# Two-layer cross-attention with gated feed-forward: the second attention layer's tiles taken two at a time, its layer norm cut into quarters

## The chip, the core and the metric

The kernel runs on one core of one Trainium2 chip. The metric is the device time of one execution in microseconds (us), as the median of a few runs. The engines are TensorE (PE in the rows; its weight loads are PEld), VectorE (DVE), ScalarE (ACT), GpSimd (POOL) and SyncE (SP), which issues every DMA here.

## The reference, cut to what matters

A model of two layers works on x of shape (32, 56, 256): 32 batches of 56 tokens. Each layer is a layer norm, a cross-attention over a context of (32, 1500, 64), a second layer norm and a feed-forward part (a mixture of 16 experts with a shared one in layer 0, a pair of routed low-rank corrections in layer 1). The change is in the attention of layer 1, which in the reference is

```python
q_hk = (hidden_q @ Wq.T).reshape(b, s, H, K)            # H = 16 heads, hidden_q = layernorm(x)
q_big = jnp.einsum('bshk,hkq->bshq', q_hk, w_kc_q)
kv_rope = kv_c * cos[None] + _rotate_half(kv_c) * sin[None]
q_r = jnp.einsum('bshq,hqr->bhsr', q_big, W_qr)
k_r = jnp.einsum('bld,hdr->bhlr', kv_rope, W_kr)
scores = jnp.einsum('bhsr,bhlr->bhsl', q_r, k_r)        # l runs over 1500 keys
attn = jax.nn.softmax(scores, axis=-1)
ctx_c = jnp.einsum('bhsl,bld->bhsd', attn, kv_rope)
ctx_lat = jnp.einsum('bhsd,hkd->bshk', ctx_c, w_kc_kv)
out = ctx_lat.reshape(b, s, H * K) @ Wo.T
```

All of it is in float32. The rotated keys depend only on the context, so layer 1 reads them from memory, where layer 0 left them.

## The kernel before

**Tiles.** The products of weights are formed once at the start of the program. In attention, a batch has 16 x 56 = 896 pairs of head and token, held as two halves of 448 columns: heads 0 to 7 on partitions 0 to 63, heads 8 to 15 on partitions 64 to 127. The 1500 keys are 12 tiles of 125. Batches go in four groups of eight (`g` is the group, `j` the batch in it, `b` = 8g + j, `t` the tile). One layer norm, one set of queries and one output projection serve a group.

**Work of one tile.** Four kinds of step make up nearly all of it.

- `score` (L953 to L963): four matmuls for each half, 64 rows deep, 125 columns of keys, 448 streamed: high parts of keys and queries, low part of the keys, low part of the queries, and a rank-one matmul (L963) that subtracts the row maximum, which lies in `shift`. They fill a wide region of PSUM (0 or 1, by turns). ScalarE then takes the exponential (L1075) into one of four buffers of `prob`.
- `mix` (L977): `prob` times the values, 125 rows deep, 64 columns for each half, two passes each, added over the 12 tiles into region 2.
- The sum of the exponentials over the tiles: GpSimd adds tiles 0 to 10 into `sums` in ten 125x896 additions (L1135), in the step `mix` of tiles 1 to 10. Step `context` adds tile 11 on VectorE (L1256). In the very last batch GpSimd takes tiles 0 to 6 only and VectorE the rest (L1243).
- `smax` (L937): the maxima for a batch still to come. They need no low parts: two halves of 500 keys against 112 queries fill region PAIR, and VectorE reduces it to its maxima (L1222). PAIR is one buffer, so a maximum's matmuls wait for the reduction of the maximum before. There are twelve a batch, four tiles ahead (`EARLY_MAX`).

**Work of one batch.** `maxneg` (L1229) negates the finished maxima, `maxT` (L943, L1062) transposes them, and SP moves them into `shift` (L861) for the next batch's scores. `norm` (L984) sums the exponentials of the batch before over its keys, ScalarE copies them out (L1088), SP packs them (L843), `spread` takes the reciprocals (L1262) and SP spreads them (L847, L852); `share` (L1286) multiplies the mixed values by them. `fetch` (L820, L822) loads the keys and values of the batch after the next. `project` (L1012) is the output projection of the group before, in batch j = 1.

**Layer norm of the next group.** `mean` (L883), `square` (L1176), `var` (L889, root on ScalarE at L1027), `rstd` (reciprocal L1181 and product L1183, in two halves of 224 columns), `xsplit` (high part on ScalarE L1033, remainder on VectorE L1188): all in batch j = 5. The eight `query` steps (six full-array matmuls, L872 to L874; L1055 and L1217 split the result) follow in batch j = 6.

**Order.** `rolling_schedule` writes one list of steps. Each engine walks through this list and executes its own part of every step, in the list's order, waiting on semaphores; SP's DMAs are issued in the same order. So the place of a step in the list is its place in every engine's queue. Before the change the order in a tile is

```python
add("score", b, t, region=t % 2)
add("mix", *old)                 # tile t - 1
if ahead[0] < NB:
    maximum(*ahead)              # four tiles ahead
```

with the steps of the batch and of the group placed between by the value of `t`. Layer 0 has a schedule of its own.

## Time and profile before

| | us |
|---|---|
| median of 3 runs | 3165.96 |
| lowest and highest run | 3162.75, 3173.43 |
| the profiled execution | 3168.89 |
| its span, from first to last instruction | 3167.1 |
| first score to last mix of the second attention layer | 963.8 |

The profile is of one execution. A window is a stretch of its span, counted in us from the span's start; busy times in it are those of each engine, and PEclk is the clock that TensorE was granted, as a share of 2.4 GHz. In a timeline the columns are start, length, engine, line of the kernel, operation, what is written and read, sizes and count; in brackets the engine's idle time before it and what ended that. Neighbouring instructions of one kind are merged, and then the length runs from the first start to the last end.

### The profile page before, as it was taken

How to read it: one execution, taken by the hardware profiler on the slowest of the kernel's cores; microseconds unless marked ns; L12 is line 12 of the kernel's file. 1: busy time of each engine (PE TensorE's matmuls, PEld its weight loads, DVE VectorE, ACT ScalarE, POOL GpSimd, SP SyncE). 2: the span in 40 equal slices, each digit the busy share in tenths (PEclk: the TensorE clock that was granted, in tenths of full speed). 3: DMA queues.
4: the chain of work that ended last, by engine and by line, in shares of the span. 5: the costliest groups of instructions: out<-in, count | busy, mean ns of one | idle time of the engine just before them, and what ended most of it. 6: DMA issues, size and time to landing. Idle time of an engine off the chain costs nothing. (4 is left out here: it accounts for less than half of the span.)

```text
span 3167.1 us, 42548 instructions
## 1 busy us (share of the span) xinstructions
PE 2853.3 (90%) x15928; PEld 1633.2 (52%) x15928; DVE 1954.6 (62%) x2322; ACT 1177.4 (37%) x1640; POOL 1668.3 (53%) x935
## 2 busy tenths in 40 slices
PE   7689899999998999996899889999999999986898
PEld 6444444444544454443788744444454454445665
DVE  2576667666766676655666556655665655636664
ACT  2124441444144423442333234444443443433331
POOL 0467775776677776771200047677676666742111
PEclk8689999999999999997899989999999999997998
DMA  8333331333133322322000143232323232300000
GB/s 288 109 84 75 87 92 34 88 76 104 36 76 84 92 58 62 75 52 85 1 1 1 28 89 80 66 78 63 75 63 75 63 75 63 83 30 23 7 6 12
DMA packets 98836, 209.15 MB, mean 66 GB/s; under 512 B 30306, under 2 KB 74322, under 8 KB 91116
## 3 DMA queue, kind: packets, MB, share of 16 engines
q1 hardware_dynamic: 98636, 206.44, 25.1%
q8 instruction: 131, 2.15, 0.3%
q14 instruction: 69, 0.57, 0.1%
HBM read 135.36 MB, written 46.00 MB: 57 GB/s over the span
## 5 line engine op out<-in xcount | busy, mean ns | idle before, releaser
L1135 POOL TENSOR_TENSOR sums<-sums,prob 125x896 f32<-125x896 f32 x556 | 1176.1, 2115 | 285.2 <-ACT prob L1075 242.2
L1222 DVE TENSOR_REDUCE maxpart<-pair 112x2 f32<-112x1000 f32 x744 | 889.9, 1196 | 451.8 <-PE pair L937 451.3
L1075 ACT ACTIVATE prob<-wide 125x896 f32<-125x896 f32 x768 | 704.4, 917 | 903.0 <-PE wide L963 901.1
L977 PE MATMUL single<-prob,kv 125*64 125x448 f32 x3072 | 753.8, 569 | 0.5
L958 PE MATMUL wide<-qhigh,kparts 64*125 64x448 f32 x3072 | 448.7, 369 | 1.5 <-DVE maxpart L1222 1.5
L937 PE MATMUL pair<-kparts,qhigh 64*112 64x500 f32 x1488 | 360.7, 481 | 88.0 <-DVE maxpart L1222 86.5
L937 PEld LDWEIGHTS pair<-kparts,qhigh 64*112 64x112 f32 x1488 | 130.1, 171 | 520.6 <-DVE maxpart L1222 440.0
L1135 POOL TENSOR_TENSOR sums<-prob 125x896 f32<-125x896 f32 x64 | 135.1, 2111 | 362.2 <-ACT prob L1075 362.2
L958 PEld LDWEIGHTS wide<-qhigh,kparts 64*125 64x125 f32 x3072 | 281.7, 184 | 79.6 <-issue 48.2
L963 PE MATMUL wide<-shift,ones_row 64*125 64x448 f32 x1536 | 284.5, 365 | 3.9 <-DMA shift<-maxrow 3.9
L958 PE MATMUL wide<-qlow,kparts 64*125 64x448 f32 x1536 | 283.0, 363 | 0.0
L977 PEld LDWEIGHTS single<-prob,kv 125*64 125x64 f32 x3072 | 152.7, 135 | 239.4 <-issue 234.9
L1096 POOL TENSOR_TENSOR w_low<-w_low_values,w_high 128x384 fp32r<-128x384 f32 (+1 forms) x72 | 74.8, 1044 | 280.1 <-ACT w_high L1038 280.1
L1120 POOL TENSOR_TENSOR sums<-prob 96x448 f32<-96x448 f32 x128 | 145.8, 1159 | 46.6 <-issue 24.0
L1864 POOL TENSOR_TENSOR ffn_hsum<-ffn_hid 128x448 f32<-128x448 f32 (+1 forms) x24 | 29.6, 1232 | 250.9 <-DVE ffn_hid L1990 250.9
L963 PEld LDWEIGHTS wide<-shift,ones_row 64*125 64x125 f32 x1536 | 144.7, 183 | 19.4 <-DMA shift<-maxrow 6.6
L958 PEld LDWEIGHTS wide<-qlow,kparts 64*125 64x125 f32 x1536 | 144.2, 183 | 13.4
L1286 DVE TENSOR_TENSOR ctx_n<-ctx_raw,recip 128x448 f32<-128x448 f32 x62 | 88.6, 1430 | 61.1 <-DMA recip<-zrec_merged 61.1
L872 PE MATMUL wide<-x_high,w_high 128*96 128x448 f32 (+1 forms) x272 | 105.9, 390 | 20.4 <-POOL w_low L1096 12.4
L1193 DVE TENSOR_TENSOR kparts<-single,kparts 64x500 fp32r<-64x500 f32 x94 | 63.0, 670 | 97.4 <-ACT kparts L1045 97.4
L1055 ACT ACTIVATE qhigh<-single 128x448 fp32r<-128x448 f32 (+3 forms) x80 | 32.0, 431 | 225.0 <-PE single L919 192.0
L1344 PE MATMUL wide<-moe_x_high,moe_wexp_high 128*128 128x448 f32 x272 | 107.8, 396 | 6.9 <-DVE moe_hid L1597 6.4
(329 smaller groups left out, 3898.2 us busy)
## 6 DMA issues: line engine op xcount, KB each, us to landing
kparts<-keys_merged SPq DMA_DIRECT2D x64, 750.0 KB, 8.9
kparts<-kparts SPq DMA_DIRECT2D x96, 250.0 KB, 3.1
keys_merged<-kparts SPq DMA_DIRECT2D x32, 750.0 KB, 7.3
recip<-zrec_merged SPq DMA_DIRECT2D x124, 112.0 KB, 2.8
w_low_values<-w_merged SPq DMA_DIRECT2D x64, 192.0 KB, 2.4
raw<-in_ctx SPq DMA_DIRECT2D x32, 375.0 KB
values_merged<-kv SPq DMA_DIRECT2D x32, 375.0 KB
kv<-values_merged SPq DMA_DIRECT2D x32, 375.0 KB
```

The costliest lines, as they stand in the source:

```text
L872: pe.matmul(dst, w_hi, x_hi, start=start, stop=False)
L937: mm = pe.matmul(acc[0:TQ, half, 0:LB], qhigh[rows_of(half), b % slots, t * TQ:(t + 1) * TQ], kparts[rows_of(half), b % 3, 0, third * LB:( ...
L958: pe.matmul(acc[0:LP, half, 0:HQ], kparts[rows_of(half), b % 3, part, cols], q[rows_of(half), b % slots, :], start=(i == 0), stop=False)
L963: mm = pe.matmul(acc[0:LP, half, 0:HQ], c["ones_row"][rows_of(half), 0:LP], shift[rows_of(half), b % 2, :], start=False, stop=True)
L977: mm = pe.matmul(mix_acc[64 * half:64 * half + DC, 0:HQ], kv[:, b % 3, t, :], prob[:, (b * LT + t) % NPROB, half * HQ:(half + 1) * HQ], st ...
L1075: nc.scalar.activation(prob[:, n_ % NPROB, :].rearrange("p (a b) -> p a b", a=2), acc[0:LP, :, 0:HQ], ACT.Exp)\
L1096: nc.gpsimd.tensor_tensor(w_low[:, h % HSLOT, :, :], w_in[:, h % HSLOT, :, :], w_high[:, h % HSLOT, :, :].bitcast(F32), ALU.subtract)\
L1120: nc.gpsimd.tensor_tensor(qr[:, h % 4, half, :], qa[:, h % 2, half, :], qb[:, h % 2, 1 - half, :], ALU.add)\
L1135: nc.gpsimd.tensor_tensor(dst, first_in, prob[:, n_ % NPROB, :], ALU.add).then_inc(s["pool_sum"], 1)
L1222: V.tensor_reduce(maxpart[:, b % 2, t:NMAX:4, third], acc[0:TQ, :, 0:LB], AX.X, ALU.max).then_inc(*R.signal_drained(kind, *key))
L1286: V.tensor_tensor(ctx_n[:, b % BG, :], ctx_raw[:, b % 2, :], recip[:], ALU.mult).then_inc(s["ctx_ready"], 1)
L1344: pe.matmul(dst, w_hi, x_hi, start=start, stop=False)
```

## The change

The second layer's schedule goes through pairs of tiles (`p` is the pair, t = 2p). In a pair the order becomes: maximum, score t, score t + 1, maximum, mix t - 2, mix t - 1. The mixes lie two tiles behind the scores, and two of them are left over after the last batch.

- Both maxima use the same region PAIR as before, the two scores regions 0 and 1.
- A query stands behind each of the two maxima, in batch j = 6, pairs 0 to 3.
- `fetch` is at the beginning of pair 1, ahead of `norm`, which is at that pair's end. `context` is at the end of pair 0, `spread` at the end of pair 3, `share` at the end of pair 5. `maxneg` is ahead of the second maximum of pair 4, `maxT` behind it.
- `project` is at the ends of pairs 2, 3 and 4, the last of them with two halves.
- The layer norm begins a batch earlier: `mean`, `square` and `var` in batch j = 4 (pairs 2, 3 and 5). In batch j = 5 the reciprocals come in four quarters of 112 columns at the ends of pairs 0 to 3 (`invert`), the products in four quarters behind the first maximum of pairs 1 to 4 (`scale`), the high part in pair 4, and the remainder in two halves in pair 5 (`xrest`), one behind the first maximum and one at the end.
- Ahead of the first batch the same quarters and halves are used. Layer 0 keeps halves (`NORM_PARTS`, `REST_PARTS`).

```diff
+NORM_PARTS = (2, 4)
+REST_PARTS = (1, KT)
...
+    def ahead(b, t):
+        n = t + EARLY_MAX
+        due = (b + 1, n) if n < LT else (b + 2, n - LT)
+        if due[0] < NB:
+            maximum(*due)
...
-    for part in range(2):
-        add("rstd", 0, part)
+    for part in range(NORM_PARTS[1]):
+        add("invert", 0, part)
+        add("scale", 0, part)
     add("xsplit", 0)
+    for k in range(KT):
+        add("xrest", 0, k)
...
-        for t in range(LT):
-            ahead = (b + 1, t + EARLY_MAX) if t + EARLY_MAX < LT else (b + 2, t + EARLY_MAX - LT)
-            if t == 2 and b + 2 < NB:
+        following = g + 1 < G
+        for p in range(LT // 2):
+            t = 2 * p
+            queries = following and j == BG - 2 and p < NPAIR // 2
+            if p == 1 and b + 2 < NB:
                 add("fetch", b + 2)
-            add("score", b, t, region=t % 2)
-            if b + 1 < NB and t == 8:
+            ahead(b, t)
+            if queries:
+                add("query", g + 1, t, region=3)
+            if following and j == BG - 4 and p == 3:
+                add("square", g + 1, 0)
+            if following and j == BG - 3 and 1 <= p <= 4:
+                add("scale", g + 1, p - 1)
+            if following and j == BG - 3 and p == 5:
+                add("xrest", g + 1, 0)
+            add("score", b, t, region=0)
+            add("score", b, t + 1, region=1)
+            if b + 1 < NB and p == 4:
                 add("maxneg", b + 1)
-            if t or b:
-                old = (b, t - 1) if t else (b - 1, LT - 1)
-                add("mix", *old)
-                if not t:
+            ahead(b, t + 1)
+            if b + 1 < NB and p == 4:
+                add("maxT", b + 1, region=3)
+            if queries:
+                add("query", g + 1, t + 1, region=3)
+            if p or b:
+                old = (b, t - 2) if p else (b - 1, LT - 2)
+                add("mix", old[0], old[1])
+                add("mix", old[0], old[1] + 1)
+                if not p:
                     add("context", b - 1)
-            if t == 1 and b:
+            if p == 1 and b:
                 add("norm", b - 1, region=3)
-            if b + 1 < NB and t == 9:
-                add("maxT", b + 1, region=3)
-            if g and j == 1 and t in (2, 3, 5, 6):
-                m, half = divmod((2, 3, 5, 6).index(t), 2)
-                add("project", g - 1, m, half, region=None if half else 3)
+            if g and j == 1 and 2 <= p <= 4:
+                for m, half in (((0, 0),), ((0, 1),), ((1, 0), (1, 1)))[p - 2]:
+                    add("project", g - 1, m, half, region=None if half else 3)
...
-            if g + 1 < G and j == BG - 2 and t < NPAIR:
-                add("query", g + 1, t, region=3)
-            if ahead[0] < NB:
-                maximum(*ahead)
-            if t == 8 and b:
+            if p == 3 and b:
                 add("spread", b - 1)
-            if t == 10 and b:
+            if p == 5 and b:
                 add("share", b - 1, 2)
+    add("mix", NB - 1, LT - 2)
     add("mix", NB - 1, LT - 1)
...
+                elif kind == "invert":
+                    g, part = key
+                    cols = slice(part * NT // norm_parts, (part + 1) * NT // norm_parts)
+                    dve.wait_ge(*R.drained("var", g))
+                    V.reciprocal(x_rstd[:, cols], x_std[:, cols]).then_inc(s["rstd"], 1)
+                elif kind == "scale":
+                    g, part = key
+                    cols = slice(part * NT // norm_parts, (part + 1) * NT // norm_parts)
+                    dve.wait_ge(s["rstd"], norm_parts * g + part + 1)
+                    V.tensor_tensor(x_n[:, :, cols], x_cen[:, :, cols], x_rstd[:, cols].unsqueeze(1).broadcast_to([128, KT, NT // norm_parts]), ALU.mult)\
+                        .then_inc(s["normed"], 1)
+                elif kind == "xrest":
+                    g, k = key
+                    dve.wait_ge(s["x_high"], g + 1)
+                    V.tensor_tensor(x_low[:, k, :], x_n[:, k, :], x_high[:, k, :].bitcast(F32), ALU.subtract).then_inc(s["x_low"], 1)
```

## Rows read from the trace of the kernel before

**Rows 1.** The page, part 1: busy time of each engine, share, instructions

```profile
PE 2853.3 (90%) x15928; PEld 1633.2 (52%) x15928; DVE 1954.6 (62%) x2322; ACT 1177.4 (37%) x1640; POOL 1668.3 (53%) x935
```

**Rows 2.** Busy time by stretch: the layer, then batches 3, 5, 6, 9, 31

```profile
1858.60:2822.40 963.80, 934.13 (x5794) 463.12 (x5794) 563.41 (x577) 420.23 (x537) 666.58 (x316) 0.99 0.28 68
1939.40:1966.34 26.94, 26.54 (x176) 13.06 (x174) 16.62 (x16) 12.34 (x15) 21.05 (x11) 1.00 0.34 82
...
1993.22:2030.00 36.78, 30.26 (x184) 14.42 (x182) 27.70 (x26) 16.39 (x19) 22.33 (x11) 1.00 0.25 60
2030.00:2068.97 38.97, 37.93 (x224) 21.44 (x222) 20.76 (x33) 17.19 (x31) 21.11 (x10) 1.00 0.23 56
2122.38:2162.14 39.76, 39.36 (x208) 18.85 (x206) 18.00 (x19) 12.34 (x15) 21.52 (x11) 1.00 0.23 55
...
2797.70:2822.40 24.70, 24.59 (x154) 10.83 (x152) 5.94 (x7) 12.22 (x15) 14.36 (x7) 1.00 0.03 10
```

**Rows 3.** Timeline of one tile, the last of batch 22

```profile
2567.63 0.48 PE L937 MATMUL pair<-kparts,qhigh 64*112 64x500 f32 x2
...
2567.95 0.57 PE L958 MATMUL wide<-qhigh,kparts 64*125 64x448 f32 x4
2568.15 1.20 DVE L1222 TENSOR_REDUCE maxpart<-pair 112x2 f32<-112x1000 f32 x1 [0.93 <-PE pair L937]
...
2568.55 0.37 PE L963 MATMUL wide<-shift,ones_row 64*125 64x448 f32 x2
...
2568.85 0.97 PE L977 MATMUL single<-prob,kv 125*64 125x448 f32 x4
2568.96 0.92 ACT L1075 ACTIVATE prob<-wide 125x896 f32<-125x896 f32 x1 [1.21 <-PE wide L963]
...
2569.76 0.48 PE L937 MATMUL pair<-kparts,qhigh 64*112 64x500 f32 x2
```

**Rows 4.** Timeline of TensorE, batch 1: a mix, a normaliser (between), a maximum

```profile
1889.03 0.97 PE L977 MATMUL single<-prob,kv 125*64 125x448 f32 x4
...
1890.68 0.48 PE L937 MATMUL pair<-kparts,qhigh 64*112 64x500 f32 x2
```

**Rows 5.** Waits in the layer: in total, times, longest

```profile
PE pair L937 <- DVE maxpart L1222: 26.6, 34, 2.6
```

**Rows 6.** Timelines of VectorE, GpSimd and ScalarE at the start of batch 3

```profile
1940.43 1.19 DVE L1222 TENSOR_REDUCE maxpart<-pair 112x2 f32<-112x1000 f32 x1
1941.54 1.08 DVE L1256 TENSOR_TENSOR sums<-prob,sums 125x896 f32<-125x896 f32 x1
...
1943.99 2.11 POOL L1135 TENSOR_TENSOR sums<-prob 125x896 f32<-125x896 f32 x1 [3.97 <-ACT prob L1075]
1946.88 8.83 POOL L1135 TENSOR_TENSOR sums<-sums,prob 125x896 f32<-125x896 f32 x4 [0.78 <-ACT prob L1075]
...
1943.00 0.92 ACT L1075 ACTIVATE prob<-wide 125x896 f32<-125x896 f32 x1 [1.14 <-PE wide L963]
```

**Rows 7.** Timelines of VectorE and GpSimd in batch 5, around a layer norm's products

```profile
2014.33 1.54 DVE L1181 RECIPROCAL x_std<-x_std 128x224 f32<-128x224 f32 x1
2015.91 2.51 DVE L1183 TENSOR_TENSOR x_n<-x_cen,x_std 128x448 f32<-128x448 f32 x1
...
2021.34 0.62 DVE L1183 TENSOR_TENSOR x_n<-x_cen,x_std 128x448 f32<-128x448 f32 x1
...
2015.86 2.08 POOL L1135 TENSOR_TENSOR sums<-sums,prob 125x896 f32<-125x896 f32 x1
```

**Rows 8.** Timeline of TensorE in batch 6: a query's first matmul, the maximum behind it

```profile
2040.35 0.47 PE L872 MATMUL single<-x_high,w_high 128*128 128x448 f32 x1
...
2041.77 0.48 PE L937 MATMUL pair<-kparts,qhigh 64*112 64x500 f32 x2
```

**Rows 9.** Timeline of SP's queue, batch 3: the fetch's first issues

```profile
1946.98 1.13 SPq L820 DMA_DIRECT2D kparts<-keys_merged  x2
```

**Rows 10.** DMA from 1939 to 1967, busy tenths in 40 slices of 0.7 us

```profile
DMA  0000000000000949998999913333100100001420
```

More of the change, by code:

```diff
@@ L126, in rolling_schedule @@
                     add("context", b - 1)
-            if t == 1 and b:
+            if p == 1 and b:
                 add("norm", b - 1, region=3)
-            if b + 1 < NB and t == 9:
-                add("maxT", b + 1, region=3)
-            if g and j == 1 and t in (2, 3, 5, 6):
-                m, half = divmod((2, 3, 5, 6).index(t), 2)
-                add("project", g - 1, m, half, region=None if half else 3)
-            if g + 1 < G and j == BG - 3:
-                if t == 2:
+            if g and j == 1 and 2 <= p <= 4:
+                for m, half in (((0, 0),), ((0, 1),), ((1, 0), (1, 1)))[p - 2]:
+                    add("project", g - 1, m, half, region=None if half else 3)
@@ L136, in rolling_schedule @@
+            if following and j == BG - 4:
+                if p == 2:
                     add("mean", g + 1, region=3)
-                if t in (3, 4):
-                    add("square", g + 1, t - 3)
-                if t == 5:
+                if p == 3:
+                    add("square", g + 1, 1)
+                if p == 5:
                     add("var", g + 1, region=3)
-                if t in (7, 8):
-                    add("rstd", g + 1, t - 7)
-                if t == 10:
+            if following and j == BG - 3:
+                if p < NORM_PARTS[1]:
+                    add("invert", g + 1, p)
+                if p == 4:
@@ L144, in rolling_schedule @@
                     add("xsplit", g + 1)
-            if g + 1 < G and j == BG - 2 and t < NPAIR:
-                add("query", g + 1, t, region=3)
-            if ahead[0] < NB:
-                maximum(*ahead)
-            if t == 8 and b:
+                if p == 5:
+                    add("xrest", g + 1, 1)
+            if p == 3 and b:
                 add("spread", b - 1)
-            if t == 10 and b:
+            if p == 5 and b:
                 add("share", b - 1, 2)
+    add("mix", NB - 1, LT - 2)
@@ L751, in attention @@
     mix_acc = region[2]
+    norm_parts, rest_parts = NORM_PARTS[layer], REST_PARTS[layer]
     steps = attention_schedule(layer)
@@ L899, in _ @@
                     pe.wait_ge(s["w_low"], NW * g + h + 1)
-                    pe.wait_ge(s["x_low"], g + 1)
+                    pe.wait_ge(s["x_low"], rest_parts * (g + 1))
                     for half in range(2):
@@ L922, in _ @@
                         pe.wait_ge(s["w_low"], h + 1)
-                        pe.wait_ge(s["x_low"], g + 1)
+                        pe.wait_ge(s["x_low"], rest_parts * (g + 1))
                         for k in range(KT):
@@ L1025, in _ @@
                     if g:
-                        act.wait_ge(s["normed"], 2 * g)
+                        act.wait_ge(s["normed"], norm_parts * g)
                     nc.scalar.activation(x_std[:], acc[:, 0:NT], ACT.Sqrt, bias=c["eps"][:, 0:1]).then_inc(*R.signal_drained(kind, *key))
@@ L1029, in _ @@
                     g, = key
-                    act.wait_ge(s["normed"], 2 * (g + 1))
+                    act.wait_ge(s["normed"], norm_parts * (g + 1))
                     if g:
@@ L1173, in _ @@
                         dve.wait_ge(s["x_high"], g)
-                        dve.wait_ge(s["x_low"], g)
+                        dve.wait_ge(s["x_low"], rest_parts * g)
                     dve.wait_ge(*(R.drained("mean", g) if k == KT - 1 else (s["cen_half"], g + 1)))
@@ L1184, in _ @@
                         .then_inc(s["normed"], 1)
-                elif kind == "xsplit":
+                elif kind == "invert":
[13 more added lines that the diff above has]
+                    V.tensor_tensor(x_low[:, k, :], x_n[:, k, :], x_high[:, k, :].bitcast(F32), ALU.subtract).then_inc(s["x_low"], 1)
+                elif kind == "xsplit" and layer == 0:
                     g, = key
```

## The prediction

> **What bounds the kernel now.** I began with the page: TensorE is busy for 90% of the span, VectorE for 62%, GpSimd for 53% [rows 1]. Only the second attention layer is edited, so the next view is the busy time by stretch. From its first score to its last mix this layer takes 963.8 us for 32 batches; TensorE is 97% busy in it, at a granted clock of 0.99 to 1.00 of the 2.4 GHz level [rows 2]. The reader should compare a plain batch (26.94 us) with those that carry the layer norm (36.78), the queries (38.97) and the output projection (39.76).
>
> Busy is not full, so the third view is the timeline of one undisturbed tile. The maximum begins at 2567.63, the score 0.32 us later, the mix 0.90 after that, the next maximum 0.90 after that: 2.13 us a tile [rows 3]. The score is four steps of two halves side by side; the last starts 0.60 to 0.61 behind the first, so together they stream for 0.81, and for 0.09 of the 0.90 nothing does. A lone mix also takes 0.90, but a mix with the normaliser behind it (same shapes, same passes) takes 1.65 [rows 4]: the normaliser costs 0.75, 0.373 a pass, with no gap, so 0.15 of a lone mix is gap. The maximum streams 500 columns where a score step has 448, hence 0.23 of its 0.32, with 0.09 of gap. The score follows the maximum (both 64 rows deep) with no more than that; the gaps stand where the shape changes to the mix's 125x64 or back. They add up to 0.34 us a tile. The last batch, which has no maxima, agrees: its 24.70 us are 12 x (0.81 + 0.75 + 0.34) + 0.75 and 1.1 of tail [rows 2].
>
> The waits view confirms that VectorE doesn't bound this: in the whole layer the maximum's matmuls wait 26.6 us for it [rows 5], and in the plain tile the reduction ends at 2569.35, 0.4 before the next maximum [rows 3].
>
> **The order.** A round is now maximum A, score, score, maximum B, mix, mix. It streams for 2 x (0.226 + 0.812 + 0.746) = 3.57 and has one pair of shape changes: 3.91, against 4.25 for two tiles before. Score behind score, maximum behind score and mix behind mix are not in the trace; each seam lies between 0 (the normaliser behind the mix, the score behind the maximum) and 0.15 (the lone mix). I take 0, since the shape stays. A's reduction starts 0.52 behind A and lasts 1.20 [rows 3], to 1.72; B's turn comes at 0.32 + 1.62 = 1.94. With its weights already loaded, B streams 0.09 sooner: reduced from 2.37 to 3.57, and the next A comes at 3.91. VectorE is left with two free places in a round, of about 0.7 and 0.85 us. Two exponentials of 0.92 fit, and prob's four buffers come free a round ahead.
>
> **The context sum.** This decides the size. Before, the 125x896 sum of L1256 ran at 1941.54, while GpSimd was idle until 1943.99, and took 1.08 [rows 6]. Now it stands behind B's reduction in a batch's first round and issues at 2.37 + 1.11 = 3.48 (1.11 lies between the two VectorE starts of [rows 6]). GpSimd's first sum needs the exponential of tile 1: the score's last step at 0.93, the exponential 0.41 later [rows 3], two of 0.92 make 3.17 at the latest, and GpSimd starts 0.07 behind it [rows 6]: 3.24. GpSimd is first, by 0.24. What follows the trace shows: a VectorE product with both inputs in SBUF, issued 0.05 after a GpSimd sum began, took 2.51 us, to 0.48 after that sum's end; alone it took 0.62 [rows 7]. So the context sum, which likewise needs all but 0.14 of its length afterwards, ends at 3.24 + 2.10 + 0.94 = 6.3. Behind it waits the next A's reduction (data at 4.43; now 6.22 to 7.42), behind that the second round's B, which loads at 7.47 and streams at 7.56, not at 3.91 + 1.94 = 5.85: 1.71 lost.
>
> A batch without collision is 6 x 3.91 + 0.75 (normaliser) + 0.19 (the transposed maxima, two passes of 0.373 x 112/448) = 24.40; a plain one becomes 26.11. The 26.94 before are 12 x 2.13 + 0.94 and 0.44 of waiting.
>
> The Trainium skill (SBUF — State Buffer, Who interferes with whom) says that such a pair excludes each other for the whole instruction and that the order of issue decides who blocks. The trace agrees in [rows 7]; with the order turned, its rule gives the first rival below.
>
> The normalised share (0.62 alone) issues 3 x 3.91 + 0.19 + 3.48 = 15.40 us after the third round begins. GpSimd's sums then come every 2.24 us (8.83 less 2.10, over 3 [rows 6]) from 2.33 on; the sixth of them ends at 15.6, so the share waits 0.2 and fits. If it lost a whole sum, the context sum would come later and wait that much less: the same total.
>
> **Layer norm.** Mean and variance are four full-array passes each: 4 x 0.373 + 0.20 (shape changes) = 1.69. They move to batch 4 of a group, where I add 0.6 for the two subtractions ahead of A's reduction and 0.5 for a square that meets GpSimd: 26.11 + 3.4 + 1.1 = 30.6. Then the square root's table loads push the first exponentials of batch 5 past 3.48, so its context sum goes first, and quarter 0's reciprocal behind it costs 0.7: a quarter lies between half and all of the 1.54 that 224 columns take [rows 7], and I take 0.84, near the half, because it has half the columns. The quarter products (half of 0.62 and a start, 0.35) stand behind A's reduction in the place of 0.7: alone they fit, behind a GpSimd sum they don't. By the 2.24 beat that costs 0.3, 0.6 and 0.15 around quarters 1 and 2, and 1.2 for quarter 3, behind which wait the maxima's negation and, on TensorE, its transpose. 24.40 + 2.95 = 27.35. Both batches: 57.95, against 26.94 + 36.78 = 63.72: 5.8 saved, three times. Bounds: 55 with no collision, 63 with each product and remainder a whole sum late.
>
> **Queries, projection, ends.** A query between mix and maximum costs 1.42 [rows 8]: six steps of 0.203 and 0.20 of shape changes. A round now has two, with three shape changes more than it has without them: 2 x 1.22 + 0.6 = 3.04, four times. 24.40 + 12.2 = 36.6, the context sum having room in rounds of 7 us: 2.4 saved, three times. Projection: 32 passes of 0.373 and three changes, 12.6, and 0.2 for its additions: 38.9, 0.86 saved, three times. Batch 0 has no context sum: 2.1 saved. Batch 30 loses its maxima after four rounds: 0.8. In batch 31 the last score starts after 5 x 3.46 + 0.75 + 0.9 = 18.95 us, not 11 x 1.90 + 0.75 = 21.65, and the VectorE chain behind it stays: 2.7. Ahead of batch 0, four short reciprocals and products stand for two long: 0.3 lost.
>
> **SP's queue.** A batch's fetch now stands ahead of the normaliser's small transfers, before behind them. The fetch issued at 1946.98 [rows 9] keeps the engines busy until about 1959.3 [rows 10], 12.3 us. Now it issues at 4.0 and is done at 16.3; the small transfer issues at 10.9. It lands between 13 (nothing in its way) and a little past the fetch's end; I take the later, 17. Its reader, the short reciprocal, issues at 17.7 and may wait until 18.6 before it delays a reduction: no cost. Each us past that costs one in 29 batches.
>
> The Trainium skill (DMA: Bandwidth & Descriptors, Queues, rings and completion order) says that an engine takes a ring's descriptors in order, which speaks for the later end. No row here shows the two in this order.
>
> **Sum.** Plain 17 x 0.83 = 14.1; layer norm 17.3; queries 7.1; projection 2.6; ends 5.6 less 0.3: 46. The profiled execution took 3168.9, 1.8 more than its span of 3167.1, and lies 2.9 above the median; 3122.5 by its time, 3120 against the median.
>
> **Rivals.** (1) The context sum issues first, or GpSimd's comes 0.25 later. For it: a margin of 0.24 out of five durations; against: these repeat from tile to tile. 1.6 comes back in 24 batches: 3082. 16%. (2) More collisions: shares, products and remainders lose whole sums, since GpSimd is now busy for 22.4 of 26 us. Half to one and a half us a batch: 3136 to 3165. 15%. (3) Slower: the gap belongs to every step whose first load carries a wait, not to the shape. For: each gap stands at such a load; against: the score behind the maximum and the normaliser behind the mix carry one too. Then 192 x 0.34 = 66 is not saved while the collisions remain: 3186; from 0.24 us of seams a round on it decides. 7%. (4) The small transfer lands later than 18.6: slower from 1.6 us beyond; 3178 at 2 us. 7%.
>
> **Numbers.** The forecast has 55%, 3106 to 3136, likeliest 3120. Low 3076 takes in (1), high 3150 most of (2): some 80%. Under 0.3% (9.5 us) a change can't be told from none. Faster: 55 + 16 + 11 of (2), 82%; within: 4 of (2) and 3 of (4), 7%; slower: 11%.
>
> **What would show it.** Eight mix matmuls in a row and rounds of 3.91; half as many idle loads ahead of the mix; L1256 at a mean near 2.6 us, with a wait of 1.7 ahead of a maximum in each second round; plain batches of 26.1, batches 5 and 6 of a group at 27.4 and 36.6. I am wrong if L1256 stays at 1.08, if score behind score shows a gap, or if the short reciprocal waits for its transfer.

## The result and the profile after

The changed kernel takes 3080.16 us (median of 4 runs, 3079.88 to 3087.07) against 3164.36 (4 runs, 3161.05 to 3173.43): a ratio of 0.9735, 95% interval 0.971 to 0.9759, 84 us less. That lies inside the range, 40 us under the likeliest value, and 2 us from the first rival (3082): the context sum is not held up by GpSimd. The page's busy times, to be read against [rows 1]:

```profile
PE 2786.6 (91%) x15928; PEld 1666.3 (54%) x15928; DVE 1952.0 (63%) x2342; ACT 1155.3 (38%) x1640; POOL 1717.0 (56%) x935
```

The busy time by stretch, as in [rows 2] (length, then busy time and instructions of PE, PEld, DVE, ACT, POOL, granted clock, DMA): the layer, then batches 2, 4, 5, 6, 9 and 31, each from its first score to the next batch's. The layer's window and that of batch 31 end at 2735.90, short of the last mix, whose row (four mixes merged) stands below them.

```profile
1856.02:2735.90 879.88, 870.24 (x5786) 499.87 (x5788) 559.17 (x592) 397.97 (x537) 715.77 (x316) 1.00 0.31 75
1907.32:1931.92 24.60, 24.60 (x177) 14.19 (x174) 16.34 (x17) 11.60 (x15) 22.68 (x11) 1.00 0.37 89
1956.92:1985.56 28.64, 28.32 (x184) 15.51 (x182) 18.69 (x20) 13.09 (x17) 25.52 (x11) 1.00 0.31 76
1985.56:2013.60 28.04, 26.31 (x182) 15.22 (x178) 23.90 (x26) 14.27 (x18) 22.88 (x11) 1.00 0.33 79
2013.60:2049.62 36.02, 35.48 (x217) 21.76 (x218) 22.27 (x33) 16.46 (x31) 20.90 (x11) 1.00 0.25 61
2098.52:2135.76 37.24, 37.24 (x208) 20.07 (x206) 17.42 (x19) 11.60 (x15) 24.29 (x11) 1.00 0.25 59
2714.26:2735.90 21.64, 21.64 (x152) 11.99 (x152) 7.63 (x7) 11.59 (x14) 16.50 (x8) 1.00 0.04 12
...
2734.23 3.23 PE L1005 MATMUL single<-prob,kv 125*64 125x448 f32 x16
```

The last mix ends at 2737.46, so from its first score to its last mix the layer takes 881.4 us where it took 963.8: 82.4 less, nearly the whole gain. The remaining 2 us are less than what the stretches ahead of the layer and behind it differ by among runs with the same code there. A plain batch takes 24.6 instead of 26.94. The six rounds of batch 1, read from the starts of the scores, are 3.92, 4.66 (with the normaliser), 3.93, 3.92, 4.11 (with the transposed maxima) and 3.93. A round of batch 3 on TensorE's timeline, beside the tile of [rows 3]:

```profile
1944.10 0.48 PE L965 MATMUL pair<-kparts,qhigh 64*112 64x500 f32 x2
1944.42 0.57 PE L986 MATMUL wide<-qhigh,kparts 64*125 64x448 f32 x4
...
1945.23 0.58 PE L986 MATMUL wide<-qhigh,kparts 64*125 64x448 f32 x4
...
1946.05 0.39 PE L965 MATMUL pair<-kparts,qhigh 64*112 64x500 f32 x2
1946.36 1.72 PE L1005 MATMUL single<-prob,kv 125*64 125x448 f32 x8
1948.02 0.48 PE L965 MATMUL pair<-kparts,qhigh 64*112 64x500 f32 x2
```

From maximum to maximum 3.92; the second score starts 0.81 behind the first, which is its streaming time, and two mixes are eight matmuls in a row. The waits of this layer, in total, times and the longest, to be read against [rows 5]:

```profile
PE pair L965 <- DVE maxpart L1265: 4.4, 11, 1.3
PE single L900 <- DVE x_low L1227: 2.6, 3, 0.9
```

Now the place that decided the size, the start of batch 3 on VectorE and GpSimd, as in [rows 6], with the record of VectorE's sequencer at the context sum's last wait (min/median/max ns, first and last start):

```profile
1933.98 1.20 DVE L1265 TENSOR_REDUCE maxpart<-pair 112x2 f32<-112x1000 f32 x1 [0.65 <-PE pair L965]
1935.10 1.08 DVE L1299 TENSOR_TENSOR sums<-prob,sums 125x896 f32<-125x896 f32 x1
1936.09 1.20 DVE L1265 TENSOR_REDUCE maxpart<-pair 112x2 f32<-112x1000 f32 x1
...
1929.42 4.57 POOL L1163 TENSOR_TENSOR sums<-sums,prob 125x896 f32<-125x896 f32 x2
1934.74 3.42 POOL L1163 TENSOR_TENSOR sums<-prob 125x896 f32<-125x896 f32 x1 [0.76 <-ACT prob L1103]
...
L1298 DVEq EVENT_SEMAPHORE  x1: 50/50/50, 1934.0 to 1934.0; - x1
```

By its record GpSimd's sum starts 0.36 us ahead of the context sum, and still the context sum runs in 1.08 and GpSimd's sum takes 3.42, until 1938.16: 1.98 us from the context sum's end. So it is in 24 of the 31 batches that follow the first (the expectations say 27, a miscount); in the sixth and seventh of the first three groups GpSimd starts later, and only in the last batch of all does the context sum lose, with 2.89. (The expectations below count from a zero 0.07 us later than the profile's: 1934.67 there is 1934.74 here.)

### The profile page after: what moved, and what is told of

Its sections match the earlier page's. It is cut to its first block and busy times, and to the rows that moved or that the text cites. A ratio compares the mean times of both kernels' runs of the same rounds, so it can differ in the third digit from the quotient of the medians.

```text
span 3078.5 us, 42568 instructions
## 1 busy us (share of the span) xinstructions
PE 2786.6 (91%) x15928; PEld 1666.3 (54%) x15928; DVE 1952.0 (63%) x2342; ACT 1155.3 (38%) x1640; POOL 1717.0 (56%) x935
## 5 line engine op out<-in xcount | busy, mean ns | idle before, releaser
L1163 POOL TENSOR_TENSOR sums<-sums,prob 125x896 f32<-125x896 f32 x556 | 1192.1, 2144 | 252.2 <-ACT prob L1103 201.8
L1103 ACT ACTIVATE prob<-wide 125x896 f32<-125x896 f32 x768 | 684.8, 917 | 779.0 <-PE wide L991 761.3
L1005 PE MATMUL single<-prob,kv 125*64 125x448 f32 x3072 | 714.0, 561 | 0.4
L965 PE MATMUL pair<-kparts,qhigh 64*112 64x500 f32 x1488 | 347.1, 462 | 65.5 <-DVE maxpart L1265 64.0
L1005 PEld LDWEIGHTS single<-prob,kv 125*64 125x64 f32 x3072 | 182.8, 135 | 249.6 <-issue 206.2
L1163 POOL TENSOR_TENSOR sums<-prob 125x896 f32<-125x896 f32 x64 | 169.0, 2641 | 264.8 <-ACT prob L1103 264.8
L900 PE MATMUL wide<-x_high,w_high 128*96 128x448 f32 (+1 forms) x272 | 106.2, 390 | 20.9 <-DVE x_low L1227 8.4
```

The costliest lines, as they stand in the source:

```text
L900: pe.matmul(dst, w_hi, x_hi, start=start, stop=False)
L965: mm = pe.matmul(acc[0:TQ, half, 0:LB], qhigh[rows_of(half), b % slots, t * TQ:(t + 1) * TQ], kparts[rows_of(half), b % 3, 0, third * LB:( ...
L1005: mm = pe.matmul(mix_acc[64 * half:64 * half + DC, 0:HQ], kv[:, b % 3, t, :], prob[:, (b * LT + t) % NPROB, half * HQ:(half + 1) * HQ], st ...
L1103: nc.scalar.activation(prob[:, n_ % NPROB, :].rearrange("p (a b) -> p a b", a=2), acc[0:LP, :, 0:HQ], ACT.Exp)\
L1163: nc.gpsimd.tensor_tensor(dst, first_in, prob[:, n_ % NPROB, :], ALU.add).then_inc(s["pool_sum"], 1)
```

## The experiments

Each kernel is the one after with one edit, but for query slot, which has two, and share behind and all three, which have three. The ratio is to the kernel before as it ran beside each of them. Total times move by several us with what lies ahead of the layer and behind it, which the edits don't touch (the first score lies between 1852.9 and 1862.2 in these runs, and from the last mix to the end it takes 337 to 347), so the column from the first score to the last is the sharper one. Even there the kernel after differs by 2.0 us between its two traces.

| run | time, us | first to last score | ratio to before, interval |
|---|---|---|---|
| before (beside the first run of after) | 3164.36 | 960.9 | |
| after | 3080.16 | 877.3 | 0.9735, 0.971 to 0.9759 |
| after, once more | 3081.03 | 879.3 | 0.9719, 0.9704 to 0.9733 |
| context sum waits late | 3114.14 | 913.3 | 0.984, 0.982 to 0.986 |
| context sum waits early | 3084.43 | 878.9 | 0.9752, 0.9727 to 0.9777 |
| four turns | 3190.69 | 989.2 | 1.0078, 1.0059 to 1.0097 |
| alternate | 3140.38 | 933.3 | 0.9916, 0.9901 to 0.9931 |
| norm in halves | 3091.60 | 888.8 | 0.9768, 0.974 to 0.9796 |
| query pairs | 3103.92 | 901.8 | 0.9807, 0.9788 to 0.9826 |
| fetch last | 3217.64 | 1012.9 | 1.016, 1.0145 to 1.0175 |
| share next | 3079.59 | 875.9 | 0.9729, 0.9706 to 0.9752 |
| query slot | 3082.51 | 875.4 | 0.9723, 0.9709 to 0.9738 |
| share behind | 3098.99 | 891.3 | 0.9769, 0.9753 to 0.9786 |
| all three | 3098.46 | 894.4 | 0.9775, 0.976 to 0.9789 |

**Who gets the port.** Theory: VectorE lays hold of the port that it shares with GpSimd when it takes an instruction up, behind the one that still runs, and not at the recorded start. Two kernels add one wait each ahead of the context sum.

```diff
                     dve.wait_ge(s["pool_sum"], pool_sums(layer, b + 1))
+                    if layer == 1 and b + 2 < NB:
+                        dve.wait_ge(*R.drained("smax", b + 2, 1, 1))     # ctx late has this line
+                        dve.wait_ge(*R.drained("score", b + 1, 0))       # ctx early has this one in its place
```

> The kernel after, with one wait more ahead of VectorE's context sum: for the end of the reduction that stands right in front of it on VectorE. The order of all instructions is as in the kernel after (span 3078.5). Theory 1: VectorE lays hold of the memory port that it shares with GpSimd when an instruction is taken up behind the running one (its waits met), not at its recorded start. In the kernel after the context sum's last wait is met at 1933.95 in the fourth batch, 0.72 us before GpSimd's first sum begins (1934.67), and so it wins although its record begins at 1935.03. With the new wait it can be taken up at 1935.11 at the earliest, GpSimd's sum is first in the 27 batches where it starts under that reduction: the context sum's record grows from 1.08 to 2.4 to 2.9 us, GpSimd's first sum shrinks from 3.41 to 2.10, the second round of these batches grows by 1.3 to 1.7 us, in all 35 to 46 us: about 3121 us. Rival: recorded starts count little because GpSimd, coming out of idle time or starting under a reduction, has no hold on the port yet: the context sum stays at 1.08, GpSimd's first sum at 3.4, and the time within 3 us of 3080.

> Control to the run with the late wait: the context sum gets one wait more here too, but for the exponential of the batch's first tile, which ends 0.9 us before GpSimd's first sum can begin (1933.76 against 1934.67 in the fourth batch) and while the reduction in front of the context sum still runs. Theory 1 (the port goes by when an instruction is taken up): nothing changes, context sum 1.08, GpSimd's first sum 3.41, 3080 us within 3. If a further wait as such costs the context sum its place: 2.4 to 2.9 us for it and about 3121 us.

VectorE and GpSimd in batch 3 with the late wait, the record of that wait, and the batch as a window:

```profile
1943.04 1.20 DVE L1265 TENSOR_REDUCE maxpart<-pair 112x2 f32<-112x1000 f32 x1 [0.65 <-PE pair L965]
1944.38 2.48 DVE L1301 TENSOR_TENSOR sums<-prob,sums 125x896 f32<-125x896 f32 x1
...
1943.81 2.10 POOL L1163 TENSOR_TENSOR sums<-prob 125x896 f32<-125x896 f32 x1 [0.84 <-ACT prob L1103]
...
L1300 DVEq EVENT_SEMAPHORE  x1: 49/49/49, 1944.3 to 1944.3; - x1
...
1940.99:1967.04 26.05, 24.72 (x178) 14.20 (x175) 17.60 (x16) 11.70 (x15) 21.25 (x11) 1.00 0.35 85
```

And with the early one:

```profile
1932.66 1.08 DVE L1301 TENSOR_TENSOR sums<-prob,sums 125x896 f32<-125x896 f32 x1
...
1932.31 3.42 POOL L1163 TENSOR_TENSOR sums<-prob 125x896 f32<-125x896 f32 x1 [0.97 <-ACT prob L1103]
...
L1300 DVEq EVENT_SEMAPHORE  x1: 49/49/49, 1931.6 to 1931.6; - x1
```

The order of instructions is the same in all three kernels. A wait met at 1944.3, behind GpSimd's start (1943.81), turns 1.08 and 3.42 into 2.48 and 2.10; a wait met at 1931.6, ahead of it (1932.31), changes nothing. The second round grows from 4.66 to 6.26 and the plain batch to a mean of 26.04, 36 us in all, 1.5 for each of the 24 batches. The rival falls: GpSimd out of idle time holds the port well enough, when it is there first.

One more rival fits these two runs: that GpSimd gets hold of the port only some time after its record starts, so that 0.36 us ahead is too little and the 0.57 with the late wait is enough. Other traces settle it. In batch 10 of the kernel after GpSimd is 0.60 us ahead by its record, out of 2.68 of idle time, and VectorE still goes first:

```profile
2139.19 1.08 DVE L1299 TENSOR_TENSOR sums<-prob,sums 125x896 f32<-125x896 f32 x1
...
2138.59 3.66 POOL L1163 TENSOR_TENSOR sums<-prob 125x896 f32<-125x896 f32 x1 [2.68 <-ACT prob L1103]
```

The context sum's last wait is met at 2138.1 there, ahead of GpSimd's start. In the run all three, below, where GpSimd goes on from one sum to the next, 0.18 us is enough for it, since the wait is met later than GpSimd's start. The same order, of the last wait's record and GpSimd's start, gives the outcome wherever a context sum meets a GpSimd sum in the kernel after and its variants.

The Trainium skill (SBUF — State Buffer, Who interferes with whom) has it that the order of issue decides which of the two blocks, and the runs agree once issue is read rightly: 1934.0 against 1934.74 in the kernel after, 1944.3 against 1943.81 with the late wait. That the two moments differ is on another page of the Trainium skill (Perfetto Trace Analysis, DVE / Act Engine Instruction): an instruction whose semaphores are met moves to a queue in front of the engine, and the profile's start comes later, when it begins to execute. The trace agrees: the context sum's start, 1935.10, lies 1.1 us behind its last wait.

**What the pairing gives.** Two kernels put single mixes back, without changing the round's contents.

```diff
             add("score", b, t, region=0)
+            if p or b:
+                add("mix", old[0], old[1])
+            ahead(b, t + 1)                            # alternate alone
             add("score", b, t + 1, region=1)
-            ahead(b, t + 1)                            # alternate alone
             if p or b:
-                add("mix", old[0], old[1])
                 add("mix", old[0], old[1] + 1)
```

> The kernel after, with the round's order maximum, score, mix, score, maximum, mix: TensorE changes between tiles of 64 and of 125 rows four times in a round instead of twice; every instruction is still there, in the same round. Theory (the gain of pairing is the gap at a change of shape, 0.34 us for a pair of changes by two tiles of 2.13 before against a round of 3.91): the plain round grows from 3.91 to 4.25, 191 rounds by 0.34 give 65 us: about 3145 us. Rival (the gap belonged to waits for the exponential or the maximum, which pairing merely spreads out): the round stays within 0.1 of 3.91 and the time within 15 us of 3080.

TensorE in batch 3 of four turns, one round and the next one's start:

```profile
1958.74 0.48 PE L966 MATMUL pair<-kparts,qhigh 64*112 64x500 f32 x2 [0.39 <-DVE maxpart L1266]
...
1962.10 0.97 PE L1006 MATMUL single<-prob,kv 125*64 125x448 f32 x4
1963.47 0.48 PE L966 MATMUL pair<-kparts,qhigh 64*112 64x500 f32 x2 [0.39 <-DVE maxpart L1266]
```

The round is 4.73: more than expected, because one mix between the second maximum and the next round's first doesn't cover the reduction, and the maximum waits 0.39. This mixes two causes, so the next run takes the wait away.

> The kernel after, with the round's order maximum, score, mix, maximum, score, mix: four changes of tile shape in a round as in the run with four turns, but with two scores and mixes of the same kind between the maxima, so that no maximum waits for the reduction of the one before it (there 0.39 us of a round of 4.73 was such a wait, and 4.34 was left). Theory (a pair of changes costs 0.35 us): the plain round is 4.26, twice the tile of the kernel before, 191 rounds by 0.35 are 67 us: about 3146 us. Rival 1 (0.43, from 4.34 against 3.91): 3161. Rival 2: the pairing gains by something else, the round stays under 4.05 and the time under 3105.

Batch 3 of that kernel:

```profile
1934.42:1960.92 26.50, 26.50 (x176) 12.97 (x174) 16.16 (x16) 12.23 (x15) 22.68 (x11) 1.00 0.35 83
```

Its rounds are 4.25 to 4.26 and the plain batch 26.49, against 3.92 and 24.61: a pair of shape changes costs 0.34, as the theory has it (3140 where 3146 was expected; the small waits of the kernel after are hidden here). The Trainium skill (TensorEngine Tiling (Array Packing), Key Properties) says that a change of tiling mode drains the engine; the two kernels agree that a change costs time, 0.34 us for a change and the change back; that the price is a drain no run here shows.

**The norm in quarters.**

```diff
-NORM_PARTS = (2, 4)
+NORM_PARTS = (2, 2)
```

and mean, squares, variance, reciprocals, products and rests at the old tiles' rounds of the sixth batch.

> The kernel after with the layer norm as it was in the kernel before: mean, squares, variance, both halves of reciprocal and product and the rest all in the sixth batch of a group (reciprocals of 224 columns, products right behind them). Theory (as the prediction sized it): the sixth batch costs what it did before beyond a plain batch, 9.8 us, and the fifth is plain, 24.45: 24.45 + 34.3 = 58.7 against the 56.7 of the kernel after, in three groups 6 us: about 3086 us. Rival 1: in rounds of two tiles a reciprocal of 1.54 and a product that waits up to 2.5 us delay two reductions in a row, 3 to 5 us more for each group: 3092 to 3100. Rival 2: the quarters bring nothing, 3080 within 3.

VectorE and GpSimd in batch 5, around the second half, and that batch as a window:

```profile
2007.49 1.54 DVE L1211 RECIPROCAL x_std<-x_std 128x224 f32<-128x224 f32 x1
2009.07 2.46 DVE L1216 TENSOR_TENSOR x_n<-x_cen,x_std 128x448 f32<-128x448 f32 x1
2011.45 1.19 DVE L1259 TENSOR_REDUCE maxpart<-pair 112x2 f32<-112x1000 f32 x1
...
2004.23 9.24 POOL L1157 TENSOR_TENSOR sums<-sums,prob 125x896 f32<-125x896 f32 x4
...
1981.53:2017.02 35.49, 30.19 (x190) 16.44 (x187) 26.16 (x28) 15.87 (x19) 25.26 (x11) 1.00 0.27 62
```

The quarters and their spreading over two batches are worth 11.5 us, twice the theory's 6 and close to the rival's lower end of 12. The product must wait for its own reciprocal, so it can't be taken up early; GpSimd, which goes through four sums in a row, is first, and a reduction comes 2 us late, as in [rows 7].

**A query behind each maximum.**

```diff
-            if queries:
-                add("query", g + 1, t, region=3)      # behind the first maximum
...
             if queries:
+                add("query", g + 1, t, region=3)      # both behind the second
                 add("query", g + 1, t + 1, region=3)
```

> The kernel after, with both queries of a round behind its second maximum instead of one behind each. Both use the same bank, so the second waits until ScalarE and VectorE have emptied it of the first: 0.6 and 0.67 us by the rows of the kernel after (query's high and low parts), and what VectorE has in front of it (a reduction of 1.2). Theory: 1.3 to 2.0 us in each of 12 rounds, 15 to 24 us: about 3098 us. Rival: the first round's query no longer waits 0.86 us for the rest of the norms, and other waits shrink: within 5 us of 3080.

TensorE's waits around the queries of the first group, in total, times, longest:

```profile
PE single L899 <- DVE qlow L1259: 5.7, 4, 1.5
PE pair L964 <- DVE maxpart L1264: 2.7, 1, 2.7
```

The layer is 24.5 us longer, with the expected wait for the bank in each of the four rounds, and a maximum behind it that waits too.

**SyncE's queue.**

```diff
-            if p == 1 and b + 2 < NB:
-                add("fetch", b + 2)
...
             if p == 1 and b:
                 add("norm", b - 1, region=3)
+            if p == 1 and b + 2 < NB:
+                add("fetch", b + 2)
```

> The kernel after, with SyncE's fetch of keys and values issued behind the small transfer of the sums in the second round, no longer ahead of it. In the kernel after the short reciprocal waits for that transfer 18 times, 19.8 us in all, but the rounds behind it are only 0.06 to 0.55 us longer than the shortest of their kind (4.10), 1.9 us in all over 8 batches. Theory (the fetch ahead of it makes the transfer late): these waits go, 2 us less, 3078 us, and no fifth round of a plain batch over 4.2. Rival: the transfer is late through its own latency; the waits stay, 3080.

A miss. The short reciprocal's waits do go, from 19.8 us and 18 times to 4.7 and one; that one is in the last batch, which has no fetch in either kernel. So the fetch was what made the small transfer late in the other 17. But the fetch now stands behind SyncE's own wait for the sums: in batch 3 it is issued 11.0 us into the batch and not 3.75, and the keys come too late for the maximum that opens the fifth round. Batch 3's wait for them, and three stretches around it:

```profile
PE pair L965 <- DMA kparts<-keys_merged: 4.5, 1, 4.5
...
1956.00:1960.50 4.50, 4.50 (x32) 2.38 (x31) 3.00 (x3) 2.32 (x3) 4.21 (x2) 1.00 0.80 174
1960.50:1965.00 4.50, 0.93 (x6) 0.14 (x2) 0.63 (x2) 0.02 (x1) 4.14 (x2) 1.00 0.85 178
1965.00:1968.00 3.00, 2.02 (x12) 2.04 (x14) 1.28 (x2) 0.01 (x1) 0.00 (x0) 0.72 0.31 114
```

7.25 us later and 4.5 of wait: by these two, the fetch of the kernel after has some 2.75 us to spare. The clock is the second part of the price: 1.00 before the pause, 0.72 in the stretch behind it, and the fifth round takes 5.68 where 4.11 is usual.

**Trying to better it.** Share next moves one product of a group, away from the remainders of the layer norm; query slot has that move and the queries one place later. Share behind and all three have the queries' move, the short reciprocal one round later, and every batch's product in the next batch:

```diff
-            if queries:                                                      # query slot, share behind, all three
-                add("query", g + 1, t, region=3)
+            if following and j == BG - 2 and 1 <= p <= NPAIR // 2:
+                add("query", g + 1, t - 1, region=3)
...
             if queries:
-                add("query", g + 1, t + 1, region=3)
+                add("query", g + 1, t, region=3)
...
-            if p == 5 and b:                                                 # share next, query slot
+            if p == 5 and b and not (following and j == BG - 3):
                 add("share", b - 1, 2)
+            if p == 0 and following and j == BG - 2:
+                add("share", b - 2, 2)
...
-            if p == 3 and b:                                                 # share behind, all three
+            if p == 4 and b:
                 add("spread", b - 1)
-            if p == 5 and b:
+            if p == 0 and b >= 2:                                            # p == 1 in all three
+                add("share", b - 2, 2)
+            if p == 5 and b == NB - 1:
                 add("share", b - 1, 2)
```

> The kernel after, with the product of the context and its reciprocals (L1329) of the sixth batch of a group moved from its last round to the first of the next batch, behind the second query. In the kernel after that product waits 1.9 of its 2.52 us for GpSimd, the reduction behind it starts late, the last round is 6.33 where no other work of TensorE is in it (3.92), and the next is 7.57 against 3.92 and two queries of 1.42. Theory: 2.0 to 2.4 us from the one round and up to 0.8 from the other, in three groups 6 to 10 us: about 3071 us. Rival: the two rests (L1227) there wait for GpSimd as before and set the end of the round, or the product takes as much in its new place: 0 to 3 us, 3078.

> The kernel after with the queries one slot later as above, so that the first of them no longer stands in front of the fifth scores of the sixth batch's end while VectorE still makes the rests of the norms (it waited 0.86 us there), and the product of the sixth batch's context and reciprocals in the next batch's first round. Theory: 1.0 us from the sixth batch's end and 0.6 from the next batch's start, in three groups 5 us: span 3073 to 3075, about 3075 us. Rival: the last query now stands in the same round as the transposed maximum, which uses the same bank, and waits there for ScalarE and VectorE: 0.7 us or more for each group, which leaves 3078.

Neither can be told from the kernel after by its total, nor by the column (1.4 and 1.9 us less, where the kernel after differs from itself by 2.0). Only the batches that the moves touch show a gain: the sixth and seventh of a group together take 64.0 to 64.1 us in both runs of the kernel after, 63.4 in share next and 63.0 in query slot. That is 1.9 and 3.1 us for three groups, of the 6 to 10 and the 5 expected. The first expectation misread a round: the 6.33 of the sixth batch's last one holds the next batch's first query (3.92 and 1.42, and 0.86 of waiting for the rests, L900 in the waits above), and stayed; only the round behind it fell, from 7.57 to 6.94.

> The kernel after with three moves: the eight queries one slot later (the first of a group behind the second maximum of its batch's first round, the last behind the first maximum of the fifth), the short reciprocal (L1305) one round later, and the product of context and reciprocals (L1329) of every batch not in the sixth round but in the first of the next batch, right behind the context sum on VectorE. Theory (the port goes by when an instruction is taken up, and to a waiting GpSimd first): GpSimd's first sum has waited since 0.35 us before the context sum began, so it comes between the two; the product takes 2.0 and 0.62, about 2.6 us, the reduction behind it starts 2.6 us later and the second round grows from 4.66 to about 7.2 in 27 batches: 70 us, less 5 to 8 from the other two moves, about 3143 us (3130 to 3150). Rival (VectorE keeps the port through instructions that follow each other): the product takes 0.62, GpSimd's first sum grows to 4.0, and the second round stays under 5.4: 3075 to 3095.

VectorE and GpSimd in batch 3:

```profile
1941.60 1.08 DVE L1301 TENSOR_TENSOR sums<-prob,sums 125x896 f32<-125x896 f32 x1
1942.60 0.62 DVE L1331 TENSOR_TENSOR ctx_n<-ctx_raw,recip 128x448 f32<-128x448 f32 x1
...
1941.25 3.94 POOL L1165 TENSOR_TENSOR sums<-prob 125x896 f32<-125x896 f32 x1 [0.78 <-ACT prob L1105]
```

The rival holds here: VectorE keeps the port for an instruction that is ready behind the first, though GpSimd has waited all the while. The second round grows by 0.52, about the product's own 0.62. In the sixth batches of the first three groups a quarter's reciprocal stands between the two; there the product waits for GpSimd (1.77 us in batch 5) and the second round takes 7.1 to 8.7 instead of 5.35.

> As the run with the product behind the context sum, but the product stands in the second round, right behind the reduction of its second maximum. Theory: it is taken up when that reduction begins (1937.83 in the fourth batch of the kernel after), ahead of GpSimd's second sum (1938.24), so it takes 0.62 us and delays nothing; the short reciprocal in the fifth round no longer waits for the small transfer (which cost 2 to 3 us in all), and with the 5 us of the query's slot: span 3069 to 3073, about 3071 us. Rival: the product waits for GpSimd there too (2 us) and the third round of every batch grows by 0.5 to 1.5: 3085 to 3120.

The product itself is not delayed (0.62 in batch 3), and the short reciprocal's rounds are 4.09 to 4.12 in every plain batch, as expected. But the context sum now loses in 8 of the plain batches. Batch 3's start, the record of the context sum's last wait, and the second rounds of batches 3, 2 and 8 as windows:

```profile
1933.41 1.20 DVE L1267 TENSOR_REDUCE maxpart<-pair 112x2 f32<-112x1000 f32 x1 [0.65 <-PE pair L967]
1934.67 2.89 DVE L1301 TENSOR_TENSOR sums<-prob,sums 125x896 f32<-125x896 f32 x1
...
L1300 DVEq EVENT_SEMAPHORE  x1: 50/50/50, 1934.6 to 1934.6; - x1
...
1927.92 6.61 POOL L1165 TENSOR_TENSOR sums<-sums,prob 125x896 f32<-125x896 f32 x3
1934.49 2.12 POOL L1165 TENSOR_TENSOR sums<-prob 125x896 f32<-125x896 f32 x1
...
1935.26:1943.56 8.30, 6.63 (x34) 2.92 (x32) 5.14 (x4) 2.39 (x4) 6.84 (x3) 0.79 0.85 187
1910.77:1915.45 4.68, 4.68 (x34) 2.56 (x32) 3.21 (x4) 2.29 (x4) 4.54 (x2) 1.00 0.85 195
2079.49:2086.08 6.59, 4.93 (x34) 2.56 (x32) 5.13 (x4) 2.39 (x4) 5.77 (x3) 1.00 0.88 191
```

In its new place the product holds up a GpSimd sum in every batch, GpSimd's chain falls behind, and its last sum of a batch ends at 1934.53, when the reduction ahead of the context sum is nearly over (1934.61). The context sum needs that sum: it is taken up only then (1934.6), when GpSimd has already gone on to the next (1934.49). The theory of the first two runs explains a loss that nobody arranged. The kernel after, run beside these:

> The kernel after itself, unchanged, beside the three runs that try to improve on it: 3080 us within 4, context sum 1.08 us and GpSimd's first sum 3.4 in 27 of 30 batches.

It took 3081.03, and no variant's total beats it by what can be measured. GpSimd's record is first and the context sum still runs in 1.08 in the same 24 batches.

## Why the prediction was right and wrong

**The order: right.** Seams of 0 and rounds of 3.91 were forecast; they are 3.92, and alternate shows that the whole difference is the shape changes. Rival 3, the gap at every step whose first load waits, falls: alternate has the same steps with the same waits and takes 0.34 more a round. Alternate also separates the rest: it costs 26.49 a plain batch, which is the 26.94 of the kernel before less the 0.44 of waiting that the forecast found in it.

**The context sum: the step that failed.** "GpSimd is first, by 0.24." By recorded starts it is first even by 0.36, so the arithmetic held; that the recorded start decides did not. [Rows 7] couldn't show it, since there the VectorE product waited for its own reciprocal and could not be taken up before it ended. What the step made of a collision was right: 26.11 was forecast for a batch with it, 26.04 is measured with the late wait, and the second round's loss is 1.60 where 1.71 was worked out. Without it the forecast was 24.40; the mean of 17 plain batches is 24.61. Taking 1.6 back in 24 batches gives the first rival's 3082, and accounts for 38 of the 40 us between the likeliest value and the measured one. So the range held because its lower end took the first rival in, at 16%, and not because the course that was thought likeliest came true. That rival spoke of the margin of starts; what carries it is another margin, between the moment when the context sum's last wait is met (GpSimd's last sum for the batch before has ended, and the reduction ahead of the context sum has begun) and GpSimd's next start. It is 0.5 to 0.8 us in those 24 batches (0.74 in batch 3), and the run all three lost it in eight.

**Layer norm.** 57.95 for both batches with one collision in it, 56.68 measured: batch 4 is 28.64 (30.6 less that collision's 1.7 is 28.9), batch 5 is 28.04 instead of 27.35. A quarter's reciprocal takes 0.84, as taken. **Queries:** 36.6 and 36.02. **Projection:** 38.9 with a collision, 37.24 without. **Ends:** the last score starts 19.06 us into batch 31, forecast 18.95; batch 0 missed, 26.83 against 27.37 before, 0.5 saved and not 2.1 (its first two rounds take 5.62 and 5.35; the cause stays open).

**SP's queue.** The fear of rival 4 was half right. The fetch does hold the small transfer: in 17 batches the short reciprocal waits for it. In batch 3 it can go 17.2 us into the batch, where 17 was taken; it is a wait because the reciprocal, without the collision that the forecast had ahead of it, is ready 1.4 us sooner. But TensorE pays for it in only seven plain batches, by 0.07 to 0.56 a round (the expectation says 8), 1.9 us in all. That is 0.11 of the 0.21 by which a plain batch's 24.61 exceeds 24.40. The first rounds behind a projection (4.17 instead of 3.91, in three of the 17 batches) make another 0.05.

## What to carry to other kernels

Put work of one tile shape together on TensorE, and leave behind each maximum enough other work to cover its reduction. When two engines share a port, ask when each instruction's last wait is met, not when its record starts: here a VectorE instruction whose inputs were ready while a reduction ran went ahead of a GpSimd sum that started later, and one that waited for its predecessor's result came behind a GpSimd sum that was ready. Before a transfer is moved behind another on the same queue, count what that queue's own waits add to it.

## What the runs showed of the hardware

- Whether the context sum or GpSimd went first at the shared port went by the moment when VectorE took the context sum up, as much as 1.1 us ahead of its record (1934.0 and 1935.10), and not by the records' starts. GpSimd's record starts although its sum is held up: 3.42 and 3.94 for a sum of 2.10.
- VectorE kept the port from the context sum to the product behind it (0.62, with GpSimd waiting). In batch 5 of the kernel after a product behind a remainder of the norms took 2.52, GpSimd coming between the two; there the first of them had itself waited for GpSimd. What makes the difference was not tried.
- A pause of TensorE can cost more than its length, and doesn't always. In the second round of batch 3 of all three it was idle for 1.67 us (8.30 less 6.63), its own busy time then rose by 1.95 over the same round in batch 2, and the mean granted clock was 0.79 of the 2.4 GHz level (0.50, the 1.2 GHz level, from 1940 to 1942). With 1.66 idle in the same round of batch 8 it stayed at 1.00. Of the eight batches with such a pause it fell in four. In fetch last, after 3.57 idle of 4.50, it was 0.72. With the late wait, 1.33 idle in a batch left it at 1.00.
